# Basis loads of a graph network cut into four transfers of one row per partition, with the rows of a group dealt out in another order

## What is computed

```
def rgcn_gate_layer(x, row, col, edge_type, basis, att, gate_w, root, bias):
    w = jnp.einsum('rb,bio->rio', att, basis)      # basis (30, 512, 512), att (2, 30)
    x_j = x[col]
    msgs = []
    for r in range(2):
        gate = jax.nn.sigmoid(x_j @ gate_w[r, :, 0])
        msgs.append(gate[:, None] * x_j @ w[r])
    msg = jnp.where((edge_type == 0)[:, None], msgs[0], msgs[1])
    agg = jax.ops.segment_sum(msg, row, num_segments=x.shape[0])
    return agg + x @ root + bias
```

## Time and profile before

| | |
|---|---|
| time, median of 3 runs | 2351.33 us (2350.43 to 2353.87) |
| time of the profiled execution | 2352.55 us |
| its span | 2350.8 us |
| TensorE matmul busy | 2202.4 us (94%) |
| VectorE busy | 1593.8 us (68%) |
| ScalarE busy | 1119.3 us (48%) |
| GpSimd busy | 546.2 us (23%) |
| moved by DMA | 189.56 MB, mean 81 GB/s |
| basis_t loads | 80 of 768.0 KB, median 12.5 us from issue to landing |

### The profile page before, as it was taken

One profiled execution on the slowest core, in us unless ns is written; L12 is line 12 of the kernel. 1 busy time (PEld: TensorE's weight loads), 2 busy tenths in 40 slices (PEclk: granted clock), 3 DMA queues, 4 the chain that ended last, 5 costly groups with the idle time before them and its releaser, 6 DMA issues.

```text
span 2350.8 us, 36257 instructions
## 1 busy us (share of the span) xinstructions
PE 2202.4 (94%) x13797; PEld 1899.8 (81%) x13797; DVE 1593.8 (68%) x3322; ACT 1119.3 (48%) x1806; POOL 546.2 (23%) x401
## 2 busy tenths in 40 slices
PE   2889968999999999999999999999999999999998
PEld 1456647899988889988888998898899888877887
DVE  9989986478776458877646887763787774244233
ACT  5146652377743347763335775233677533222321
POOL 6000000066510026650003663000566200000000
PEclk9899978999999999999999999999999999999999
DMA  9899963111031011003102003111110421062034
GB/s 253 220 250 253 274 203 123 44 31 44 1 113 66 21 52 44 22 37 101 52 20 65 22 23 98 64 37 31 44 44 1 134 73 29 17 103 43 1 69 105
DMA packets 110945, 189.56 MB, mean 81 GB/s; under 512 B 57893, under 2 KB 58341, under 8 KB 103099
## 3 DMA queue, kind: packets, MB, share of 16 engines
q1 hardware_dynamic: 106776, 180.47, 28.9%
q10 hardware_dynamic: 4003, 6.79, 1.1%
HBM read 155.16 MB, written 32.07 MB: 80 GB/s over the span
## 4 chain that ended last, share of the span: by engine, by line
PE 75%; DVE 11%; issue 5%; ACT 5%; DMA 2%; DVEq 1%; SPq 1%; POOL 0%; ACTq 0%; POOLq 0%
PE PS L1043 10%; PE PS L1071 9%; PE PS L962 6%; PE PS L964 6%; PE PS L963 6%; PE PS L1057 6%; PE PS L948 5%; PE PS L952 4%; PE PS L949 4%; PE PS L1199 4%; PE PS L1209 4%; PE PS L859 3%; PE PS L812 2%; ACT prob L1433 1%; DMA basis_t<-in_L_gnn_basis_dram 1%
## 5 line engine op out<-in xcount | busy, mean ns | idle before, releaser
L793 POOL TENSOR_SCALAR prob<-prob,inv_den 125x1000 f32<-125x1000 f32 x160 | 444.5, 2778 | 0.0
L781 POOL TENSOR_TENSOR rstd<-var_eps,neg_half 125x2 f32<-125x2 f32 x45 | 35.4, 787 | 907.1 <-DVE var_eps L1596 907.1
L1433 ACT ACTIVATE prob<-prob,neg_max 125x1254 f32<-125x1254 f32 x160 | 215.5, 1347 | 56.9 <-DVE neg_max L1936 56.7
L1931 DVE CUSTOM_DVE_ANT_0 prob<-PS,sbias 125x1254 f32<-125x1254 f32 x160 | 233.0, 1456 | 11.0 <-issue 8.4
L1071 PE MATMUL PS<-pT_hi,v_hi 125*128 125x250 f32 x800 | 236.0, 295 | 0.0
L1950 DVE TENSOR_TENSOR pT_lo<-PS,pT_hi 125x1000 fp32r<-125x1000 f32 x160 | 191.1, 1194 | 51.2 <-ACT pT_hi L1450 51.2
L1071 PE MATMUL PS<-pT_lo,v_hi 125*128 125x250 f32 x800 | 224.1, 280 | 0.0
L1071 PE MATMUL PS<-pT_hi,v_lo 125*128 125x250 f32 x800 | 222.3, 278 | 0.0
L1057 PE MATMUL PS<-ident,prob 125*125 125x125 f32 x1600 | 201.7, 273 | 5.6 <-DVE pT_lo L1953 5.5
L1057 PEld LDWEIGHTS PS<-ident,prob 125*125 125x125 f32 x1600 | 196.1, 189 | 12.6 <-issue 7.6
L1448 ACT ACTIVATE pT_hi<-PS 125x1000 fp32r<-125x1000 f32 x160 | 161.8, 1011 | 82.7 <-PE PS L1057 82.7
(11 more groups left out here) (330 smaller groups left out, 5628.2 us busy)
## 6 DMA issues: line engine op xcount, KB each, us to landing
basis_t<-in_L_gnn_basis_dram SPq DMA_DIRECT2D x80, 768.0 KB, 12.5
sbias<-score_bias SPq DMA_DIRECT2D x40, 548.6 KB
adj<-adj SPq DMA_DIRECT2D x20, 546.9 KB
w_lo_raw<-in_L_gnn_m_w_dram SPq DMA_DIRECT2D x8, 1024.0 KB, 6.5
score_bias<-biases SPq DMA_DIRECT2D x10, 548.6 KB
adj<-count SPq DMA_DIRECT2D x10, 546.9 KB
xc<-x_lat SPq DMA_DIRECT2D x12, 448.0 KB
x_first<-x_lat SPq DMA_DIRECT2D x10, 448.0 KB
```

Source lines behind the costliest of these rows:

```text
L793: pool.tensor_scalar(prob[u % 3][:, 0:SPLIT], prob[u % 3][:, 0:SPLIT], inv_den[0:T, u % 4:u % 4 + 1], None, ALU.mult)\
L1433: act.activation(prob[u % 3][:], prob[u % 3][:], ACT.Exp, bias=neg_max[0:T, u % 4:u % 4 + 1], accum_out=den[0:T, u % 4:u % 4 + 1]).then_in ...
L1931: v.tensor_tensor_reduce(prob[u % 3][:].rearrange("p (j s) -> p j s", j=3), PS[0:T, 0:3, 0:SB], sbias[p % 2][a][:].rearrange("p (j s) -> p ...
```

## The change

Each basis load becomes four transfers, one for each j, of 96 partitions by one row (2 KB). In the same step row 16j + i of a group now goes to partition position i as its j-th row, so that the 16 positions of one transfer are 16 neighbouring rows of a matrix. TensorE waits for four transfers where it waited for one. load_r undoes the new order: it reads rel_w as (j, i).

```
@@ load_r
                         sp.dma_start(wr_raw[n][p0:p0 + GR, k // 2, :],
-                                     rel_w[l, k, :, :].rearrange("(j r i) d -> r i j d", j=4, r=R)[n]).then_inc(rel_in[n], 16)
+                                     rel_w[l, k, :, :].rearrange("(j r i) d -> r j i d", j=4, r=R)[n]).then_inc(rel_in[n], 16)
@@ load_bases
                 rows = (basis1, basis2)[l].rearrange("(b g) a d -> g b a d", g=NBG)[g][:, GR * k:GR * (k + 1), :]
-                sp.dma_start(basis_t[n % RING][:], rows.rearrange("b (i j) d -> i b (j d)", j=4)).then_inc(basis_in[n % RING], 16)
+                for j in range(4):
+                    sp.dma_start(basis_t[n % RING][:, j, :], rows[:, GROUP_I * j:GROUP_I * (j + 1), :].rearrange("b i d -> i b d"))\
+                        .then_inc(basis_in[n % RING], 16)
@@ relation_loads
-                    pe.wait_ge(basis_in[load % RING], 16 * (load // RING + 1))
+                    pe.wait_ge(basis_in[load % RING], 64 * (load // RING + 1))
```

## The result

Slower. The changed kernel takes 2370.3 us (median of 4 runs, 2364.8 to 2372.9), the kernel before, run beside it, 2352.6 (4 runs, 2350.4 to 2354.7). The ratio is 1.0082, 95% interval 1.0063 to 1.0101, so 14.8 to 23.8 us more. The prediction said 2362, slower, range 2346 to 2388. The profiled execution is the fastest of the four, 2364.8 us with a span of 2363.0.

The account below looks back on a forecast made before the run. The prediction took the sort to wait for the basis stream and the count to be held by VectorE, DMA close behind. It summed -8 (stream), +17.3 (load_r) and +1 (first place) to +10, forecasting 2362 us, range 2346 to 2388.

Parts of the forecast that it names:

- load_r on four engines: Relation-weight loads: the source's new outermost count of four confines each transfer to four DMA engines instead of 16.
- Rival A: load_r keeps 16 engines because the destination's 64 decide; only the stream's -8 remains, 2343 us; chance 0.15.
- Its price: Start of the first aggregation: load_r ends later, so root and adj land later, +17.3 us (bounds +10.8 and +31.8).
- Two of the signs: At the first aggregation: adj landing over 25 us after issue, TensorE idle over 20 us.
- Rival B: load_r's four engines run at full pace, 24.3 GB/s each: +10.8, first place 0, stream -8, 2354 us; chance 0.17.
- The first place: Behind the last attention block: eight load_r transfers ahead of the xc loads make xc late, +1 us (0 to +8).
- The stream: Basis loads in sort and count: about 300 GB/s instead of 255 shortens TensorE's waits, -8 us.
- Rival C: The basis stream gets slower, below 233 GB/s, so the count waits too; 2391 us at 220 GB/s; chance 0.13.
- The issues at 0: SyncE's queue: 240 more issues at 562 ns, 135 us of a mostly waiting engine, cost 0.
- The 54 GB/s: load_r: if its four engines shared ports in two pairs, 54 GB/s and 38.8 us, so +28.

Follow-up runs that it names:

- x2: Kernel before with only load_r's read order changed to (j, i), basis loads as before: 2370.3 us, ratio 1.0074.
- y1: Changed kernel, but load_r reads 16 rows into 16 partitions, four such rows a partition, in eight transfers: 2351.5 us, ratio 0.9998.
- z1: The kernel before, unedited, run and profiled once more: 2352.9 us (one run).
- x1: Kernel before with only the basis loads changed, load_r as before: 2351.1 us, ratio 0.9992.
- x3: Kernel before with four basis transfers of one row per partition, old dealing of rows and old load_r: 2351.1 us, ratio 0.9999.
- z2: Kernel before, but from the seventh basis load on only one of a partition's four rows is loaded: 2350.2 us, ratio 0.9987.
- x4: Kernel before with two basis transfers of two rows per partition (4 KB pieces), old dealing and load_r: 2345.3 us (one run).
- w2: Kernel before with four one-row basis transfers, old dealing, second layer's old load_r in three portions behind adj tiles 3, 5, 7: 2340.6 us, ratio 0.9940.
- w3: Kernel before with the second layer's load_r in three portions behind adj tiles 3, 5 and 7: 2345.4 us, ratio 0.9956.

## Why the prediction was right, and where its terms were off

**load_r on four engines: right.** The share of 0.26, the x2 kernel that loses all of it and the y1 kernel that loses nothing show it. Rival A, where the 64 partitions decide, is out.

**Its price was mis-sized, +17.3 for +13.1.** I took 18.6 GB/s for an engine, from transfers with pauses between them, and set the 24.3 of the 125-row loads as the lower bound. It is 24.5, at the bound. That alone was worked out as +10.8. Tiles 0 to 2 took 48.6 us with the new load_r (after, x2) and 35.45 with the old one (before, z1): +13.1. The waits of TensorE carry this: 18.7 and 18.0 us against 5.4 and 5.4. The rest over +10.8, some 2 us, I take for the shares of root and adj that stood behind load_r on its four engines: from 2074 to 2080 us the DMA share is once more 0.26, and from 2080 to 2084 it is full, before adj lands at 2084.1. Full share at a low rate (150 GB/s from 2070 to 2074) is no sign of it, since the kernel before has that too while root and adj run, 138 GB/s from 2068 to 2072. That is argued, no run took it apart. Two of the signs came out smaller than stated: adj landed 17.3 us after its issue and not over 25, and TensorE stood for 18.7 us and not over 20. Rival B had this pace right, and the sum wrong for the next two reasons.

**The first place was mis-sized, +1 for +5.3, within its 0 to +8.** From load_r to the aggregation the four profiles with the new load_r give 204.3 on the mean (203.9 to 204.7), the ten others 198.9 (198.1 to 199.7), 5.3 less before rounding. I had counted when load_r ends, and not what stands with it in the engines' queues: xc is issued 5.8 us behind the first load_r (1850.25) and lands 15.51 us later, in stretches at full share that move 226 to 228 GB/s, 14 an engine. With 24.5 an engine the eight transfers alone, 1.05 MB, would have been through in 10.7 us, so the pace of load_r isn't what failed; that xc's own shares on four engines stood behind load_r's is the reading that fits, and was not tested by itself. VectorE's wait accounts for 5.9 of the 6.6 us of the changed kernel; the little that is left may be the clock, which I had not counted: behind the longer wait TensorE is granted 0.72 to 0.74 from 1866 to 1878 us in these four profiles, and 1.00 in before.

**The stream: the mechanism right, the size -8 for -4.** The sort no longer waits for it, and it goes at 302 to 319 GB/s where I had said 300. Against before's own profile the gain is 8.1, as worked out. But that profile was late by chance: the five with old loads end the count at 449.7, 445.6, 445.5, 446.7 and 446.7, mean 446.9; the seven with four transfers at 441.4 to 444.5, mean 442.6. So -4.2. The waits of the earlier trace rows were thus partly that one profile's. Rival C is out.

**The sum.** -4.2 + 5.3 + 13.1 = +14.2, against +17.7 by the medians and +14.8 to +23.8 by the interval. That the forecast of 2362 came within 8.3 us owes something to luck: load_r's 4.2 too much and the first place's 4.3 too little cancel, and what is left of the miss is the stream's 3.8 and the 3 to 4 us that the sum does not reach. x2 alone has 5.3 + 13.1 = 18.4, and measured +17.4. So in the medians of the changed kernel the stream's gain doesn't show, as it doesn't in x1, x3 and y1. In those three a part is met at tiles 0 to 2, which took 37.9 to 40.2 us against 35.1 and 35.8; z2, with a quarter of the stream, has 37.5. In these four adj took 10.8 to 14.1 us to land, against 9.1 to 9.2 in before, z1 and x4. In y1 its own slow load_r is the likely reason. In x1, x3 and z2 load_r lands as in before (2.7 to 2.8 us at the median), but root is already late, 9.0, 8.8 and 7.1 us from issue to landing against 6.3, 5.8 and 5.8 in before, z1 and x4. Why it is, 1600 us behind the last basis load, stays open; the difference of w2 and w3, which don't wait there, would fit this place as where the gain goes. In the changed kernel itself (48.7, x2 48.5) nothing was taken there. Its missing 3 us may be the clock: its profile is the fastest of its four runs (span 2363.0, mean granted clock 0.979) and took none of the slow stretch in the rest, and the other three have 2366.8 to 2371.0 at 0.978 and 0.977. They have no profile, so it isn't shown; and four runs of it and five of x2 don't tell 4 us well.

**The issues at 0: right in the stream, wrong at load_r.** 320 basis issues at 597 ns held nothing up. But the eight of wv took 9.28 us for 4.5, as SyncE had to wait for the four engines. That I hadn't counted; the adj load is issued 5.2 us later for it, relative to load_r. It is no price on top, for the engines would not have been free sooner.

## What to carry to other kernels

When a transfer's order is changed, look at what stands outermost on both of its sides, not at its bytes or its addresses; a share of 0.26 in a stretch with one kind of transfer is the sign. Then look at what is queued behind that transfer, in time and on its engines: here 2 MB that nothing was waiting for yet cost 13 us through the one tile behind them, and putting them between tiles gave more than any load order did. And take the waits of one profile as one throw: two profiles of one kernel ended the stage 4 us apart whose waits the gain was worked out from, and differed by 3 us at another place through the clock alone.

## What the runs showed of the hardware that was not expected

- Loads into 96 partitions, 80 to 116 us, go faster when they are cut up: 259 to 276 GB/s with one transfer of 8 KB pieces (five profiles), 290 with two of 4 KB (one), 299 to 307 with four of 2 KB in six profiles and 287 in a seventh, at a full DMA share each time and whichever rows are neighbours.
- Few engines are each fast: 24 GB/s with four at work (102 to 107 at a share of 0.26 to 0.28). With all sixteen busy it depends on the transfers: 16 to 19 in the basis loads (259 at 1.02, 319 at 1.06), 14 behind the last attention block (226 to 228), 6 to 8 where root and adj run together (138 at 1.41, 150 at 1.11).
- The 54 GB/s that the prediction had worked out for four engines into 64 partitions, from a sharing of ports, was not met: 102 to 107. But sixteen engines into 16 neighbouring partitions a transfer, y1, gave only 8 to 11 GB/s each, 144 to 150 together, where the same bytes into 64 partitions gave 18.6 each before. Why was not tested.
- An issue on SyncE takes about 0.55 us, and 0.9 to 1.5 us when the engines it feeds are behind (eight in 9.28 us).
- A wait of 1.8 us was followed by some 6 us of TensorE at half clock in z1 and by none in before, in one and the same kernel; the stage took 3.1 us more for it.
